# Folding the linear attention's weights during the routing of layer 0 instead of among its experts

## The reference, cut to what matters

```python
h = rmsnorm(x, attn_norm_w)
q, k, v = h @ Wq, h @ Wk, h @ Wv            # 8 heads of 128
attn = where(causal, q_h @ k_h.T, 0)        # per chunk, and a running state
o_h = rmsnorm(attn @ v_h + q_h @ S, attn_out_norm_w)
x = x + concat(o_h) @ Wo
```

## Time and profile before

| | us |
|---|---|
| median of 3 runs | 954.49 (953.7 to 958.48) |
| profiled execution | 959.48 |
| its span in the trace | 958.0 |
| attention's part of the span | 0 to 479 |
| `attention_output` | 479.8 to 499.5 |
| routing of layer 0 | 499.9 to 516 |
| experts of layer 0, to the last scatter | 516 to 563 |
| results back and norm | 564 to 580 |

### The profile page before, as it was taken

How to read it: one execution, slowest core, us unless ns; L and a number is a source line. 1 busy time by engine, 2 the same in 40 slices (tenths; PEclk the granted TensorE clock), 3 DMA queues, 4 the chain that set the end, 5 groups by cost and what they waited for, 6 DMA issues and landing times. The chain is left out here.

```text
span 958.0 us, 25373 instructions
## 1 busy us (share of the span) xinstructions
PE 780.9 (82%) x10797; PEld 464.3 (48%) x10797; DVE 605.5 (63%) x1412; ACT 484.0 (51%) x974; POOL 220.0 (23%) x239
## 2 busy tenths in 40 slices
PE   6386999999999999999863958999998696026990
PEld 4012555555555555554442944666664354024770
DVE  3797769788878978780065232767676544762444
ACT  5522778787787778788831543434343222001222
POOL 3983121111121121212203724000000000005631
PEclk9555899999999999999965976999999797556995
DMA  5561215141314121000076126200000002201104
GB/s 190 147 228 61 66 27 76 26 77 30 71 35 72 33 68 38 4 3 5 2 233 175 49 61 227 72 1 1 2 1 1 0 1 67 69 0 39 40 26 143
DMA packets 45747, 59.08 MB, mean 62 GB/s; under 512 B 11924, under 2 KB 22877, under 8 KB 45632
## 3 DMA queue, kind: packets, MB, share of 16 engines
q1 hardware_dynamic: 42512, 51.47, 20.4%
q0 software_dynamic: 2304, 4.74, 1.9%
q10 hardware_dynamic: 816, 1.23, 0.4%
HBM read 42.09 MB, written 15.07 MB: 60 GB/s over the span
## 5 line engine op out<-in xcount | busy, mean ns | idle before, releaser
L800 DVE CUSTOM_DVE_ANT_0 junk<-row,rest 128x1024 bf16<-128x1024 f32 x256 | 307.8, 1223 | 60.4 <-PE row L421 47.1
L649 ACT ACTIVATE prob<-score 128x512 f32<-128x512 f32 x512 | 278.5, 612 | 85.7 <-PE score L421 81.0
L421 PE MATMUL score<-stack 75*32 75x128 bf16 (+3 forms) x3840 | 204.9, 300 | 5.7 <-DMA stack<-neg_rows 1.3
L514 PE MATMUL out_ps<-prob,v_aug 128*32 128x256 f32 x2048 | 153.9, 384 | 1.9 <-ACT prob L649 1.9
L421 PE MATMUL row<-stack 72*32 72x512 bf16 x1792 | 140.6, 389 | 2.1 <-DVE top L800 1.5
L421 PEld LDWEIGHTS score<-stack 75*32 75x32 bf16 x3840 | 91.9, 97 | 95.1 <-ACT prob L649 17.6
L736 POOL TENSOR_SCALAR_AFFINE_SELECT prob<-prob 128x512 f32<-128x512 f32 x64 | 40.6, 634 | 295.7 <-ACT prob L649 295.7
L514 PEld LDWEIGHTS out_ps<-prob,v_aug 128*32 128x32 f32 x2048 | 61.4, 111 | 38.6 <-ACT prob L649 3.3
L421 PEld LDWEIGHTS row<-stack 72*32 72x32 bf16 x1792 | 47.2, 98 | 35.4 <-issue 5.0
L1945 PE MATMUL outs<-vm_w,mixed 128*64 128x256 f32 x512 | 61.7, 381 | 1.8 <-issue 1.8
L1426 PE MATMUL up_ps<-rows_t,up_w 128*128 128x320 f32 (+1 forms) x192 | 60.0, 438 | 1.4 <-DVE rows_t L1638 1.2
(11 more groups left out here) (312 smaller groups left out, 1058.3 us busy)
## 6 DMA issues: line engine op xcount, KB each, us to landing
stack<-parts_dram SPq DMA_DIRECT2D x288, 64.0 KB
parts_dram<-prob SPq DMA_DIRECT2D x12, 256.0 KB, 3.2
parts_dram<-stack SPq DMA_DIRECT2D x12, 256.0 KB, 3.0
results<-x_tok SPq DMA_DIRECT2D x12, 256.0 KB, 3.6
up_w<-in_L_ffn_w_dram SPq DMA_DIRECT2D x1, 2048.0 KB, 9.6
rows<-x_tok SPq DMA_DIRECT2D x8, 256.0 KB, 3.7
y<-results SPq DMA_DIRECT2D x8, 256.0 KB, 4.2
up_w<-in_L_ffn_wg_dram SPq DMA_DIRECT2D x1, 2048.0 KB, 11.3
```

The source lines that it names most:

```text
L421: last = pe.matmul(out[c:c + 32, :], keys[:, c:c + 32], queries, start=True, stop=True)
L514: last = pe.matmul(out_ps[at:at + 32, part * (S // 4):(part + 1) * (S // 4)], v_aug[g.third][:, tile, h, :], moving[:, 2 * part:2 * part + ...
L649: act.activation(prob[tile % 2][:, h, part * HALF:(part + 1) * HALF], score[n % NS][:, :], ACT.Exp).then_inc(exped, 1)
L800: dve.tensor_tensor_reduce(junk[:, n % 2, :], row[n % 2][:, :], rest[:, S - P - tile * P:2 * S - P - tile * P], 1.0, LOWEST, ALU.mult, ALU ...
```

## The change

The loads of the linear attention's weights move in SyncE's order from behind the store of `share` to the place between the routing's constants and the expert weights, one stage earlier. The scaling moves from VectorE to GpSimd, to the end of its program in `attention_output`; for w_v it writes straight into `vm_w`, which saves ScalarE one copy per head. TensorE's turning and folding leaves the expert loop and stands in three pieces of the routing; ScalarE's copies stand in two pieces. Turned weights and products get two banks each. TensorE waits for all copies before it turns the first gathered rows. Everything else is as it was.

```diff
             load_route_constants(sp, mem, io)
+            load_linear_weights(sp, mem, io)
             load_expert_weights(sp, mem, io, 0)
...
             pool.memset(mem["router0"][:, E:32], 0.0).then_inc(mem["router_set"], 1)
+            scale_weights(pool, mem)
...
         down_ps = [ps(f"down_ps{i}", [P, 512]) for i in range(2)]
-        folding = weight_folding(sb, sem, norm_ps) if layer == 0 else None
+        folding = weight_folding(sb, sem, norm_ps, (down_ps[0], xturn_ps[0])) if layer == 0 else None
         logit_ps, turn_ps = xturn_ps[0], xturn_ps[1][:, :].rearrange("p (j c e) -> p j c e", j=4, c=4)
...
             last.then_inc(routed, 1)
+            if folding:
+                fold_stages(pe, mem, folding, 0, 2)
...
             cumulate(layer, True).then_inc(cum_out, 1)
+            if folding:
+                fold_stages(pe, mem, folding, 2, 4)
...
             last.then_inc(owners_out, 1)
+            if folding:
+                fold_stages(pe, mem, folding, 4, H1 + 1)
...
+            if folding:
+                pe.wait_ge(folding["f_copied"], H1)
             for c in turns_at(0):
...
                         up(e, c)
-                    if folding and e and c == 0:
-                        fold_weights(pe, mem, folding, e - 1)
-                    if folding and e < E and c == 1:
-                        turn_weights(pe, mem, folding, e)
                     if e and 0 < c <= len(of(e - 1)):
...
                     c = t // 4
-                    if t == 0:
-                        pe.wait_ge(folding["f_copied"], E)
                     if t < NT - 2:
...
             act.activation(e_x[:, :, :], left[:, :, :], ACT.Exp).then_inc(exped, 1)
+            if folding:
+                copy_weights(act, mem, folding, 0, 4)
             act.wait_ge(tiles_in, 1)
...
                                scale=mem["column"][:, k:k + 1]).then_inc(visits_in, 1)
+            if folding:
+                copy_weights(act, mem, folding, 4, H1 + 1)
...
                     act.activation(hidden[e % 2][:, c, :], up_ps[n % 2][0][:, 0:cap], ACT.Gelu_apprx_tanh).then_inc(h_in, 1)
-                    if c == 2:
-                        copy_turned_weights(act, mem, folding, e)
-                    if c == 1 and e:
-                        copy_folded_weights(act, mem, folding, e - 1)
                 else:
...
                     act.activation(acted[:, n % 2, :], up_ps[n % 2][0][:, 0:cap], ACT.Silu).then_inc(acted_in, 1)
-            if folding:
-                copy_folded_weights(act, mem, folding, E - 1)
             act.activation(warm[:, :], mem["column"][:, 0:1], ACT.Sqrt)
...
                 turned_rows(c)
-            if folding:
-                scale_weights(dve, mem, folding)
             for e in range(E + 1):
...
             sp.dma_start(rows_p[:, :, D:D + E], share[:, :, :]).then_inc(share_stored, 16)
-            if layer == 0:
-                load_linear_weights(sp, mem, io)
             sp.wait_ge(stored, 16 * (NT // 4))
...
-def weight_folding(sb, sem, banks):
...
-    fold = {n: sem("lw_" + n) for n in ("scaled", "turned", "t_copied", "folded", "f_copied")}
+def weight_folding(sb, sem, turn_banks, fold_banks):
...
+    fold = {n: sem("lw_" + n) for n in ("turned", "t_copied", "folded", "f_copied")}
     fold["turned_w"] = sb("turned_w", [P, 2, 3, P])
-    fold["turn_ps"] = banks[0][:, 0:3 * P].rearrange("p (n e) -> p n e", n=3)
-    fold["fold_ps"] = banks[1][:, 0:2 * D].rearrange("p (n d) -> p n d", n=2)
+    fold["turn_ps"] = [bank[:, 0:3 * P].rearrange("p (n e) -> p n e", n=3) for bank in turn_banks]
+    fold["fold_ps"] = [bank[:, 0:2 * D].rearrange("p (n d) -> p n d", n=2) for bank in fold_banks]
     return fold
-def scale_weights(dve, mem, fold):
...
-    dve.wait_ge(mem["linear_in"], LINEAR_LOADS)
+def scale_weights(pool, mem):
...
+    pool.wait_ge(mem["linear_in"], LINEAR_LOADS)
     for n in "qkvo":
         w, k = mem[f"w_{n}"], int(n != "o")
-        dve.tensor_scalar(w[:, :, :], w[:, :, :], mem["norm_w"][:, k:k + 1], None, ALU.mult).then_inc(fold["scaled"], 1)
+        into = mem["vm_w"][:, :, 0:D] if n == "v" else w[:, :, :]
+        pool.tensor_scalar(into, w[:, :, :], mem["norm_w"][:, k:k + 1], None, ALU.mult).then_inc(mem["linear_scaled"], 1)
...
     if h == 0:
-        pe.wait_ge(fold["scaled"], 4)
-    else:
-        pe.wait_ge(fold["t_copied"], h)
-    for k, n in enumerate("qkv"):
-        last = pe.transpose(fold["turn_ps"][:, k, :], mem[f"w_{n}"][:, h, :], mem["ident"][:, :])
+        pe.wait_ge(mem["linear_scaled"], 4)
+    if h >= 2:
+        pe.wait_ge(fold["t_copied"], h - 1)
+    for k, w in enumerate((mem["w_q"], mem["w_k"], mem["vm_w"])):
+        last = pe.transpose(fold["turn_ps"][h % 2][:, k, :], w[:, h, 0:D], mem["ident"][:, :])
     last.then_inc(fold["turned"], 1)
...
-    turned_w, fold_ps = fold["turned_w"], fold["fold_ps"]
+    turned_w, fold_ps = fold["turned_w"], fold["fold_ps"][h % 2]
     pe.wait_ge(fold["t_copied"], h + 1)
-    if h:
-        pe.wait_ge(fold["f_copied"], h)
+    if h >= 2:
+        pe.wait_ge(fold["f_copied"], h - 1)
     pe.matmul(fold_ps[:, 0, :], turned_w[:, h % 2, 0, :], turned_w[:, h % 2, 1, :], start=True, stop=True)
     pe.matmul(fold_ps[:, 1, :], turned_w[:, h % 2, 2, :], mem["w_o"][:, h, :], start=True, stop=True).then_inc(fold["folded"], 1)
...
+def fold_stages(pe, mem, fold, begin, end):
...
+    for h in range(begin, end):
+        if h < H1:
+            turn_weights(pe, mem, fold, h)
+        if h:
+            fold_weights(pe, mem, fold, h - 1)
...
         act.wait_ge(fold["folded"], h - 1)
-    act.copy(fold["turned_w"][:, h % 2, :, :], fold["turn_ps"][:, :, :]).then_inc(fold["t_copied"], 1)
+    act.copy(fold["turned_w"][:, h % 2, :, :], fold["turn_ps"][h % 2][:, :, :]).then_inc(fold["t_copied"], 1)
...
-    a_w, vm_w = mem["a_w"], mem["vm_w"]
     act.wait_ge(fold["folded"], h + 1)
-    act.copy(a_w[:, h, :], fold["fold_ps"][:, 0, :])
-    act.copy(vm_w[:, h, 0:D], mem["w_v"][:, h, :])
-    act.copy(vm_w[:, h, D:2 * D], fold["fold_ps"][:, 1, :]).then_inc(fold["f_copied"], 1)
+    act.copy(mem["a_w"][:, h, :], fold["fold_ps"][h % 2][:, 0, :])
+    act.copy(mem["vm_w"][:, h, D:2 * D], fold["fold_ps"][h % 2][:, 1, :]).then_inc(fold["f_copied"], 1)
...
+def copy_weights(act, mem, fold, begin, end):
...
+    for h in range(begin, end):
+        if h < H1:
+            copy_turned_weights(act, mem, fold, h)
+        if h:
+            copy_folded_weights(act, mem, fold, h - 1)
...
         mem["r_in"] = [sem(f"r_in{t}") for t in range(E * C1 // P)]
+        mem["linear_scaled"] = sem("linear_scaled")
         mem["linear_in"], mem["mlp_in"], mem["mlp_scaled"] = sem("linear_in"), sem("mlp_in"), sem("mlp_scaled")
...
             route_constants(nc, mem, io, sb, keep)
+            mem.update(a_w=sb("a_w", [P, H1, D]), vm_w=sb("vm_w", [P, H1, 2 * D]))
             attention_output(nc, mem, io)
-            mem.update(a_w=sb("a_w", [P, H1, D]), vm_w=sb("vm_w", [P, H1, 2 * D]))
             mem.update(h_tok=sb("h_tok", [P, NT, D]), h_t=sb("h_t", [P, T]))
```

## The result

The changed kernel takes 959.68 us (median of 20, 955.3 to 965.32), the kernel before beside it 955.02 (median of 20): ratio 1.0051, 95% interval 1.0033 to 1.007. It is slower by half a per cent, where a small gain was forecast, and it lies outside the range of 948.9 to 957.5. The profiled execution has a span of 960.0 against 958.0 us.

What follows compares the result with a forecast made beforehand. It took GpSimd's descriptor work and TensorE, close together, to bound the expert loop, with routing waiting for VectorE and ScalarE at the barrier. Terms: -5.5 + 3.9 = -1.6 us, median 952.9, range 948.9 to 957.5.

Steps and rivals of the forecast that it cites:

- term 3: `attention_output`: four GpSimd scalings at 1.09 us each block VectorE's `tensor_scalar`; barrier 3.9 us late, between 0.4 and 7.8.
- 4P - 0.5: `attention_output`: the barrier's delay in us if each GpSimd scaling of price P blocks VectorE for its whole length.
- Rival C: `attention_output`: scalings stretch or cost more than the product; at P = 3.2, +6.8 us, 961.3; chance 0.10.
- Term 1: Layer 0 expert loop: TensorE's period falls from 4.51 to 3.94 us, GpSimd then limits; 5.5 us less.
- Term 2: Routing: folding costs nothing; full clock near 519, first `up` at 522.5, TensorE keeps up with GpSimd.
- Term 4: Transfers: earlier loads and the later store of `share` are hidden under the late barrier; uncovered, about 1 us.
- Term 5: VectorE's four scalings and ScalarE's eight copies of w_v leave engines that wait anyway: 0.
- The last step of the prediction: Whole kernel: carried the profiled execution's 5.0 us above the median over, giving 954.49 - 1.6 = 952.9.

Runs made afterwards that it cites:

- e3: Changed kernel with each GpSimd scaling as a product of two tensors (column broadcast) instead of `tensor_scalar`; ratio 1.0086 to the kernel before.
- g2: Changed kernel again, no edit, in the fifth batch; ratio 1.0077 to the kernel before.
- e10: Changed kernel again, no edit, in the third batch; ratio 1.0082 to the kernel before.
- e12: Kernel before with only the linear attention weights' loads moved ahead of the expert weights; ratio 0.9982 to the kernel before.
- e2: Changed kernel with the four scalings on VectorE at the start of its routing program, folding left in the routing; ratio 1.0002 to the kernel before.
- f1: Kernel before with 80 more transposes on TensorE ahead of h_tok's transposes, in the wait for the results; ratio 1.0 to the kernel before.
- e9: Kernel before, unchanged, timed against itself and profiled as a control; ratio 0.9994.
- e4: Kernel before with loads early and scaling on GpSimd before the barrier, folding left among the experts; ratio 1.0071 to the kernel before.
- e5: Kernel before, unchanged, profiled as a control in the second batch; layer 0 loop 54.04 us, no ratio given.
- f2: Changed kernel with scaling on VectorE at the routing's start and `share` stored by ScalarE; ratio 0.9928 to the kernel before.
- g1: Changed kernel with scaling on VectorE at the routing's start and `share` stored by ScalarE, repeated in another batch; ratio 0.9981 to the kernel before.
- e7: Changed kernel with three scalings (q, k, v) at VectorE's end of `attention_output`, w_o's left on GpSimd; ratio 1.0002 to the kernel before.
- e6: Changed kernel with all four scalings at VectorE's end of `attention_output` instead of on GpSimd; ratio 1.0037 to the kernel before.
- f3: Changed kernel with scaling on VectorE at the routing's start, `share` stored by ScalarE, and 80 more TensorE transposes; ratio 0.9953 to the kernel before.
- f4: Changed kernel with GpSimd's scalings of w_q, w_k, w_o over half their columns; half width 1.56 to 1.58 us each, `attention_output` 23.70.
- e1: Changed kernel again, no edit, in the first batch; ratio 1.0079 to the kernel before.
- e8: Changed kernel with GpSimd's four scalings multiplying by the constant 1.0 instead of the column; 2.76 to 2.79 us each, `attention_output` 27.10.
- e11: Changed kernel with 64 one-column matmuls more on TensorE at the start of `attention_output`; they take 26.46 us, loop 49.65.

## Why the prediction was wrong

**The step that failed is the price in term 3**, "I take 1.09, since a scaling reads one tensor like the select". A scaling takes 2.84, above even the upper bound of 2.08, and the barrier is 7.0 us late instead of 3.9. With those 3.1 us less the measured median would be 956.6, inside the range. Both neighbours were of other operations: the same work as a product of two operands takes 1.89, as `tensor_scalar` 2.84 (e3). The bound could not hold, since nothing in the trace of before said that a one-input operation costs no more than a two-input one. It wasn't even one for two inputs: it was doubled from half the size, while products of the full size are in that trace, at 2.12 to 3.25 us. Two of its groups of GpSimd:

```profile
L676 POOL TENSOR_TENSOR prob<-y,v_aug 128x1024 f32<-128x1024 f32 x2 | 6.5, 3254 | 16.8 <-DVE prob L771 16.8
L685 POOL TENSOR_TENSOR prob_late<-stack 128x1024 f32<-128x1024 f32 x2 | 4.2, 2120 | 0.0
```

The page "GPSIMD Engine Reference" of the Trainium skill, section "Elementwise — side-by-side cycle accounting", gave an estimate of 1.54 us, nearer than the select and still half of what these runs show.

**The blocking in term 3 is real, but not for this instruction.** Beside products VectorE gets one instruction in for each (e3), as the memset of the earlier trace rows had shown. This agrees with what "SBUF — State Buffer" of the Trainium skill, section "Who interferes with whom", states. Beside GpSimd's `tensor_scalar` it loses 0.5 to 1.4 us in a group of four (1.75 and 1.70 instead of 1.11, in g2 2.48) and 0.5 to 0.9 in a `var` (0.67, in e10 1.02, instead of 0.17), never a whole 2.84; for that the section's "fully blocks" is too strong in these runs. Why the two operations of GpSimd differ in this, no run shows. The delay of the barrier is therefore not 4P - 0.5, which at P = 2.84 would be 10.9, but that of GpSimd alone: from the landing at 496.20, four times 2.84 and 0.3 to the barrier at 507.86, against 500.87 for the old length of the stage; 7.0. Rival C had the right sign and the wrong sum: at P = 2.84 it gives +5.4 us and 959.9, which the measured 959.68 meets by luck, for the stages around the change give +2.3.

**Term 1** gave -4.7 instead of -5.5. The reason is in its own small stall, 0.31 us where 0.21 was reckoned: the period is 4.04 instead of 3.94, so TensorE and not GpSimd ends the loop, and before the last scatters GpSimd is idle for 0.65, 0.35 and 1.08 us where 0.30 is usual. Up to 559 gathers and scatters are 1.25 to 1.33 apart behind the first, as said. **Term 2** holds: routing is 16.34 in both, the folding in it free. The first gather is 8.1 us later than before, so the clock, expected at 519, should rise at 527.1; it is 0.50 in 524 to 526 and 0.68 in 526 to 528, which puts the rise near 527.3. The first `up` stands 6.1 us behind the first gather, where the prediction had 6.4. **Term 4**: hidden in the changed kernel, since the barrier is late. Without that cover it costs 0.54 (e12) to 0.58 (e2); the term said "about 1 us". ScalarE's issue takes most of it away (16.52 and 16.34). **Term 5** holds.

**The sum by measured terms** is +7.0 - 4.7 = +2.3, the profiles' +2.0 (with 1.1 more in attention, 0.8 less between, and the rest), but 4.7 in the medians. The last step of the prediction, "the same difference on the median", took the profiled execution as typical outside the stages in question. It was 4.5 above the median of the 20 executions timed beside the changed kernel, and above all of them; that of the changed kernel was 1.8 above its own median. What stood apart in it may be linear attention: it took 226.91 us, and in the four later profiles of the kernel before or of its variants e12 and f1 it takes 222.7 to 223.2. The changed kernel has 226.4, 226.9, 226.5 and 225.1 in its four.

The difference is in the clock. In e9 it is 0.72 from 2 to 4 us behind the start of linear attention (583.23) and then full; in e10 (start 592.07) it is 0.50 until 600:

```profile
585.00:587.00 2.00, 1.60 (x18) 1.35 (x15) 0.00 (x0) 0.95 (x2) 1.92 (x3) 0.72 0.77 270
587.00:589.00 2.00, 1.71 (x10) 0.78 (x10) 0.53 (x1) 0.22 (x1) 1.92 (x3) 1.00 0.90 221
...
598.00:600.00 2.00, 2.00 (x10) 1.24 (x8) 1.09 (x3) 0.00 (x0) 1.92 (x3) 0.50 0.91 291
600.00:602.00 2.00, 2.00 (x10) 0.38 (x8) 0.09 (x1) 0.59 (x1) 2.00 (x3) 0.81 1.02 370
```

This first rise is not all of it. In every profile the clock falls to half again about 160 us into the stage, and once more at its end, and these stretches differ in length too. The time at half clock, worked out from the shares (length times twice what is missing from 1.00), and the length of the stage in all 20 profiles:

| profiles | at the start | about 160 us in | at the end | sum | linear attention |
|---|---|---|---|---|---|
| e4, e5, e9, e12, f1, f2, g1 | 3 to 4 | 10 | 3.5 | 17 | 222.7 to 223.2 |
| e2, e7 | 8 | 10 | 3.5 | 22 | 224.4, 224.6 |
| e6, f3, f4, g2 | 4 | 14 | 6 | 24 | 225.1 |
| before, changed, e1, e3, e8, e10, e11 | 9 | 14 | 6 | 28 to 29 | 226.4 to 226.9 |

The stage is the longer the longer it is at half clock, without an exception. A long sum is no property of the changed kernel: the first profile of the kernel before has it too, and most of its executions in the batch of f1 to f4 have the low mean clock.

With linear attention the third batch (e9, e10) comes near its medians: 7.3 (`attention_output`) - 2.2 (loop) + 3.7 (linear attention) + 0.9 (routing 1) - 0.5 (the rest) = 9.2 by stages, 8.2 by the medians. Attention's 3.6 us between these two profiles are left out here, and e9's profile is the fastest of its 12 executions, so this fits but proves nothing. In the first pair, 20 executions each, 2.4 of the 4.7 us of the medians lie outside `attention_output` and the loop. That they are the clock's is likely by the table and not shown: the clock of the unprofiled executions of the kernel before is not known there.

**What stays open**: what makes these stretches long or short, which the one edit that was to touch it (f1) didn't settle; and what the stalls are. The stalls are in every profile of four batches and in none of f1 to f4 or of the first pair. One of the four batches ran on the same chip number as f1 to f4, so the chip alone is not their cause; their number and first place go with where the folding stands. That the changed kernel's gain in the loop is smaller where they are (2.2 us by e9 and e10, 4.7 without them) is shown, their source is not.

**What the change is worth without its scaling on GpSimd.** With the folding in the routing and the scaling on VectorE the ratios are 0.9928 and 0.9953 without the stalls (f2, and f3 with its 80 transposes), and 0.9981, 1.0002 and 1.0037 with them (g1, e2, e6). The scaling on GpSimd costs 7.0 us of `attention_output`, and moving it away gives them back (e2). That the rest of the change then gains is shown only for the batch without stalls, where a higher clock has its part in it.

## What to carry to other kernels

An engine that is idle is not free if its work ends at a barrier: before moving work to GpSimd, find the same operation, not a like one, in a trace, and where there is none let the price range over a factor of three. Compute separately when the moved work itself is done and when it lets the other engine be done; the later one sets the stage. And before a difference between two profiles is carried over to medians, see whether the profiled execution lies where its median lies, and compare the time at half clock in each stage that the change doesn't touch.

## What the runs showed of the hardware

- On GpSimd 128x1024 float32 takes 2.84 us as `tensor_scalar` with a column, 2.77 with a constant, 1.89 as a product with a broadcast column; 1.09 was a select. VectorE does the first in 0.74.
- GpSimd's products of 1.89 us let one `tensor_scalar` of VectorE through each (a `var` took 1.54 us instead of 0.17, four `x_tok` 5.75 instead of 1.11); beside GpSimd's `tensor_scalar` of 2.84 the four took 1.64 to 2.48. In the other direction a cast of 0.29 us took 0.75 beside VectorE's scalings.
- 64 float32 matmuls of one column took 26.46 us (e11), 0.41 each at half clock, where eight transposes of 128x128 took 1.97, 0.25 each, at half clock in the same stage of the changed kernel.
- With 2 MB more of loads before them and the barrier at its old place SyncE's four stores of `rows` take 7.1 to 7.4 us to issue (e2, e12, f2, g1) instead of 2.3; with the barrier 1.7 us later 5.35 (e6), and 2.33 in the changed kernel, where it is 7.0 later.
- Linear attention of the kernel before took 222.8 to 226.9 us, with 17 to 29 us of it at half clock: 4.1 us, more than the 2.3 that the change's own stages add up to.
